# Writing out the loops of an attention and expert kernel, and moving its weight waits and splits to other engines

## The reference

```
x = x + autocorrelation(layernorm(x), ctx, ctx)
x = x + moe(layernorm(x))

autocorrelation, 8 heads of 64 channels, over the 64 positions of each channel:
  corr = ifft(fft(q) * conj(fft(k))).real
  w, idx = top_k(corr, 8);  w = softmax(w)
  out = sum over i of w_i * v shifted by idx_i   (index clamped at the last position)

moe, 16 experts, top 2:
  shared = (silu(x @ Wg.T) * (x @ Wu.T)) @ Wd.T             (512 -> 2 * 512 -> 512)
  two experts of each token by softmax(x @ gate.T), weights normalised to sum 1
  out = sum over both of weight * expert(x) + shared        (expert: 512 -> 2 * 128 -> 512)
```

## Time and profile before

| | us |
|---|---|
| median of 3 runs | 550.24 |
| lowest and highest run | 548.26, 551.55 |
| the profiled execution's own time | 549.62 |
| its span in the trace | 547.8 |
| PE busy | 448.0 (82%) |
| DVE busy | 307.2 (56%) |
| POOL busy | 295.6 (54%) |
| ACT busy | 266.9 (49%) |

### The profile page before, as it was taken

One profiled execution on the slowest core, in us unless ns is written; L12 is line 12 of the kernel. 1 busy time (PEld: TensorE's weight loads), 2 busy tenths in 40 slices (PEclk: granted clock), 3 DMA queues, 4 the chain that ended last, 5 costly groups with the idle time before them and its releaser, 6 DMA issues.

```text
span 547.8 us, 9530 instructions
## 1 busy us (share of the span) xinstructions
PE 448.0 (82%) x2320; PEld 343.5 (63%) x2321; DVE 307.2 (56%) x940; ACT 266.9 (49%) x527; POOL 295.6 (54%) x340
## 2 busy tenths in 40 slices
PE   4699888988988899999905877787777878799995
PEld 3355655655655557788705766676666767588884
DVE  3898989889899836793301322332323323247656
ACT  5688888887888835312002434344444444322120
POOL 3357677777777764097773447474445400056631
PEclk9899999999999999999956999999999999799999
DMA  5522344454542422138876466676666443157854
GB/s 201 245 64 91 121 149 134 134 167 168 184 152 96 155 63 66 46 119 304 283 274 212 145 230 201 210 247 200 219 215 211 125 143 115 40 174 232 251 157 146
DMA packets 39270, 91.58 MB, mean 167 GB/s; under 512 B 4432, under 2 KB 4432, under 8 KB 39120
## 3 DMA queue, kind: packets, MB, share of 16 engines
q1 hardware_dynamic: 32256, 64.31, 35.4%
q0 software_dynamic: 6992, 27.01, 15.1%
HBM read 49.88 MB, written 41.42 MB: 167 GB/s over the span
## 4 chain that ended last, share of the span: by engine, by line
PE 38%; POOL 22%; issue 18%; ACT 8%; DVE 7%; DMA 5%; POOLq 0%; ACTq 0%; DVEq 0%; SPq 0%
PE bank L452 29%; PE bank L602 6%; POOL xs_rows L1251 4%; POOL arena L1167 3%; POOL arena L1170 3%; POOL act_lo L1198 3%; POOL tokens_lo L1154 2%; DMA xg_sb<-xs_rows 2%; POOL rstd L1147 2%; ACT act_lo L721 1%; POOL shw_lo L1202 1%; DMA xs_rows<-x2T,pos_i 1%; ACT arena L776 1%; ACT arena L775 1%; ACT arena L777 1%
## 5 line engine op out<-in xcount | busy, mean ns | idle before, releaser
L1069 DVE TENSOR_TENSOR tokens_lo<-bank,tokens_hi 128x512 fp32r<-128x512 f32 x47 | 32.5, 692 | 89.7 <-ACT tokens_hi L810 89.7
L602 PE MATMUL bank<-const_sb,xg_sb 128*128 128x128 f32 x188 | 31.5, 291 | 58.5 <-issue 38.3
L810 ACT CAST tokens_hi<-bank 128x512 fp32r<-128x512 f32 x47 | 27.6, 587 | 87.8 <-PE bank L602 87.8
L1275 POOL DMA_INDIRECT arena<-y_rows,pos_i x32 | 32.4, 1013 | 66.8 <-DMA y_rows<-sh_act 43.8
L1225 POOL CAST w_hi<-x2T 128x1536 fp32r<-128x1536 f32 x16 | 23.6, 1476 | 74.8 <-PE bank L452 72.2
L602 PEld LDWEIGHTS bank<-const_sb,xg_sb 128*128 128x128 f32 x188 | 20.4, 144 | 68.1 <-issue 67.2
L452 PE MATMUL bank<-tokens_hi,shw_hi 128*128 128x512 f32 x128 | 51.9, 406 | 5.7 <-DVE tokens_lo L878 3.8
L1227 POOL TENSOR_TENSOR w_lo<-x2T,w_hi 128x1536 fp32r<-128x1536 f32 x16 | 55.7, 3481 | 1.3
L452 PE MATMUL bank<-w_hi,tokens_hi 128*128 x188 | 54.1, 288 | 0.2 <-issue 0.2
L452 PE MATMUL bank<-w_hi,tokens_lo 128*128 x188 | 53.5, 285 | 0.0
L452 PE MATMUL bank<-w_lo,tokens_hi 128*128 x188 | 53.5, 284 | 0.0
(11 more groups left out here) (145 smaller groups left out, 1243.6 us busy)
## 6 DMA issues: line engine op xcount, KB each, us to landing
xg_sb<-xs_rows SPq DMA_DIRECT2D x47, 256.0 KB, 2.7
y_rows<-sh_act SPq DMA_DIRECT2D x47, 256.0 KB, 2.1
xs_rows<-act_lo SPq DMA_DIRECT2D x10, 1024.0 KB, 5.1
x2T<-w_exp POOLq DMA_DIRECT2D x13, 768.0 KB, 4.5
resid<-x SPq DMA_DIRECT2D x16, 256.0 KB, 4.7
arena<-ctx SPq DMA_DIRECT2D x16, 256.0 KB, 4.9
x_rows<-arena SPq DMA_DIRECT2D x16, 256.0 KB, 2.1
x2T<-x_rows SPq DMA_DIRECT2D x16, 256.0 KB, 4.2
```

Source lines behind the costliest of these rows:

```text
L602: last = nc.tensor.transpose(ps_xgT[:, cols], xg[b][:, cols], C["identity"])
L810: copy(xgT_halves[b][0], ps_xgT[:, :]).then_inc(xgT_hi_ready, 1)
L1069: tt(lo, ps_xgT[:, :], hi.bitcast(F32), ALU.subtract).then_inc(xgT_ready, 1)
L1275: nc.gpsimd.indirect_dma_start(y_in[buf], None, y_rows[:, :], bass.IndirectOffsetOnAxis(ap=pos_i[:, col:col + 1], axis=0)).then_inc(y_gath ...
```

## The change

- The loops of all engines are written out. `iteration` and `expert` get their numbers as constants.
- The wait for a tile's weights moves from PE to DVE. DVE loads the tile's word (`weights_of`), waits for `w_ready`, and increments a new semaphore `weights_there`; PE waits for that by a constant. It stands at the end of DVE's `expert(n)`, behind the `lo` half of tile n-1's activation (which waits for ACT's `hi` half of it), and is for tile n+1. PE loads a tile's word once and keeps the register for the down product.
- The shared expert's weights are loaded one iteration earlier and are split by POOL alone, in n = 1 to 12: the cast (`split_hi`) behind `keep`, the subtraction (`split_lo`) between the two steps of `odd_product`. The tokens of group 0 are split in the same two places, in n = 13 (tile 0), n = 14 (tiles 1 and 2) and n = 15 (tile 3, here with the cast behind L1189).
- The first three experts' weights are loaded into the place of their own `lo` half, early, and `bounce` is loaded early. POOL splits expert 0 before the scatter, DVE splits experts 1 and 2 beside it. POOL makes the first two `lo` halves of group 0's shared activation, DVE those of group 1's tokens. So the scatter stands behind expert 0's split, instead of behind expert 0's, group 1's tokens' and expert 1's.
- DVE finds the maxima and indices of 15 of the 16 router tiles before the last one's logits are there, and makes the `lo` halves of group 0's third activation behind the positions instead of between their steps.
- POOL loads experts 3 and 4 right behind the scatter (before, behind expert 2's split).
- At the end of the tiles, `shared_half(2, 0, 0)` stands behind the last two down products. The tokens of group 2 are split in four places between tiles 44 and 47 instead of at one.

The diff, cut to its core:

```diff
-                if n == 0:
+                if n == -1:
                     sp.dma_start(shw_in[:, :], shw[:, :]).then_inc(shw_loaded, 16)
...
-            with eng.Fori(hs.start, hs.stop) as h:
-                for b in range(2):
-                    iteration(h, b, None)
+            for n in range(-2, PAIRS + 3):
+                iteration(n // 2, n % 2, n)
...
+            sp.wait_ge(tokens_lo_ready, GT)
+            for t in range(BOUNCES):
+                sp.dma_start(bounce[t], x2_rows[t * P:(t + 1) * P, :]).then_inc(bounced[t], 16)
+            for e, free in enumerate((w_even_psum, out_psum, x2T_psum)):
+                sp.wait_ge(free, PAIRS)
...
+                sp.dma_start(w_raw[e], w_exp[:, e * EXPERT:(e + 1) * EXPERT]).then_inc(weight_first[e], 16)
...
-                pe.wait_ge(w_ready, word % WORD)
+            def gate_up(j, at):
+                b = j % 2
+                pe.wait_ge(weights_there, j + 1)
                 pe.wait_ge(xgT_ready, j + 1)
...
+            def weights_at(j):
+                return pe.value_load(tile_word[0:1, j:j + 1], min_val=1, max_val=(RING - 1) * EXPERT * WORD + E) // WORD
+            def expert(n):
+                b = n % 2
+                if n + 1 < SLOT_TILES:
+                    at[n + 1] = weights_at(n + 1)
+                if n + 2 < SLOT_TILES:
+                    transposes(n // 2 + 1, b)
+                if 1 <= n <= SLOT_TILES:
+                    pe.wait_ge(act_ready, n)
+                    wait(pe, actT_ready, n - 1)
                     nc.tensor.transpose(ps_actT[:, 0:P], act_sb[1 - b][:, :], C["identity"]).then_inc(actT_psum, 1)
+                if n >= 2:
+                    pe.wait_ge(actT_ready, n - 1)
+                    wait(pe, y_ready, n - 3)
+                    down_at = at[n - 2] + KB * 2 * INTER
                     split_product(ps_y[b][:, :], actT_halves[b],
...
+                if n + 1 < SLOT_TILES:
+                    gate_up(n + 1, at[n + 1])
...
-            shared_half(2, 0, 0)
-            for n in range(SLOT_TILES, SLOT_TILES + 2):
-                expert(n // 2, n % 2, n)
+            for n in range(SLOT_TILES + 2):
+                if n == 0:
+                    pe.wait_ge(sh_added, 2 * GT)
+                expert(n)
             for m in range(SB):
                 for part in range(2):
-                    if m or part:
-                        shared_half(2, m, part)
+                    shared_half(2, m, part)
...
-                if n is None or 2 <= n < 2 + SHW // D:
-                    chunk = 2 * h + b - 2
-                    act.wait_ge(shw_loaded, 16)
-                    copy(tile_of(shw_hi, chunk), tile_of(shw_in, chunk)).then_inc(shw_hi_ready, 1)
...
+            def split_weights(e):
+                slot = slice(e * EXPERT, (e + 1) * EXPERT)
+                dve.wait_ge(weight_first[e], 16)
+                dve.wait_ge(w_ready, e)
+                nc.vector.tensor_copy(w_hi[:, slot], w_raw[e]).then_inc(w_hi_ready, 1)
+                dve.wait_ge(w_hi_ready, e + 1)
+                tt(w_lo[:, slot], w_raw[e], w_hi[:, slot].bitcast(F32), ALU.subtract).then_inc(w_ready, 1)
...
-            for t in range(PAIRS):
-                last = nc.vector.max(vals[:, t], log_t[:, t])
+            for tiles in (range(PAIRS - 1), range(PAIRS - 1, PAIRS)):
+                dve.wait_ge(logits_ready, tiles.stop)
+                for t in tiles:
+                    last = nc.vector.max(vals[:, t], log_t[:, t])
...
+            act_lo_split(0, 2)
             shared_multiply(0, 3)
             act_lo_split(0, 3)
+            for t in range(GT):
+                tokens_lo_split(1, t)
...
             for m in range(SB):
                 shared_multiply(1, m)
                 act_lo_split(1, m)
+                if m < 2:
+                    split_weights(m + 1)
...
+            def weights_of(j):
+                word = dve.value_load(tile_word[0:1, j:j + 1], min_val=1, max_val=(RING - 1) * EXPERT * WORD + E)
+                dve.wait_ge(w_ready, word % WORD)
+                dve.sem_inc(weights_there, 1)
...
                     dve.wait_ge(actT_hi_ready, j)
                     hi, lo = actT_halves[1 - b]
                     tt(lo, ps_actT[:, 0:P], hi.bitcast(F32), ALU.subtract).then_inc(actT_ready, 1)
+                if n + 1 < SLOT_TILES:
+                    weights_of(n + 1)
...
+            def split_hi(n):
+                if 1 <= n <= SHW // D:
+                    pool.wait_ge(shw_loaded, 16)
+                    nc.gpsimd.tensor_copy(tile_of(shw_hi, n - 1), tile_of(shw_in, n - 1)).then_inc(shw_hi_ready, 1)
+                for t in split_tokens(n):
+                    pool.wait_ge(x2T_kept, t + 1)
+                    pool.wait_ge(shw_lo_ready, SHW // D)
+                    nc.gpsimd.tensor_copy(tile_of(tokens_hi, t), tile_of(x2T, t)).then_inc(tokens_hi_ready, 1)
...
+            def split_tokens(n):
+                return {PAIRS - 3: (0,), PAIRS - 2: (1, 2), PAIRS - 1: (3,)}.get(n, ())
...
                     nc.gpsimd.tensor_tensor(w_odd_sw, w_odd_sw, ctx_odd_im[pb], ALU.mult).then_inc(odd_im_products, 1)
+                    split_lo(n)
                     pool.wait_ge(out_products_ready, 2 * p + 2)
...
+            pool.wait_ge(xs_zeroed, 16 * (PAIRS - 5))
+            act_lo_split(0)
+            pool.wait_ge(out_products_ready, 2 * PAIRS)
             split_weights(0)
-            for t in range(GT):
-                tokens_lo_split(1, t)
-            split_weights(1)
+            act_lo_split(1)
...
-            split_weights(2)
             for buf in range(BOUNCES):
                 pool.wait_ge(scattered[buf], 16 * CHOICES * PAIRS // BOUNCES)
+            load_weights(4)
+            pool.wait_ge(tokens_lo_ready, 2 * GT)
             load_weights(3)
-            pool.wait_ge(w_ready, 3)
-            load_weights(4)
```

More of the change, by code:

```diff
@@ L331, in segs @@
             return ap.rearrange("p (s l) -> p s l", s=SEGS)
-        def schedule(iteration):
-            for i in range(-2, 4):
-                iteration(i // 2, i % 2, i)
-            return range(2, (PAIRS - 2) // 2), [(i // 2, i % 2, i) for i in range(PAIRS - 2, PAIRS + 3)]
         def live(n, d):
-            return n is None or 0 <= n + d < PAIRS
+            return 0 <= n + d < PAIRS
         def pair(h, b, d):
@@ L429, in _ @@
                 load_xg(j // 2, j % 2)
[L430 to L435 removed]
+            for j in range(6, SLOT_TILES):
+                load_xg(j // 2, j % 2)
+                store_y((j - 6) // 2, j % 2)
+            for j in range(SLOT_TILES - 6, SLOT_TILES):
                 store_y(j // 2, j % 2)
[L437 removed]
+            for t in range(PAIRS):
                 sp.wait_ge(y_added, t + 1)
@@ L832, in _ @@
             act.wait_ge(sh_out_psum, 2 * GT)
-            for n in range(4):
-                expert(n // 2, n % 2, n)
-            with act.Fori(2, SLOT_TILES // 2 - 1) as h:
-                for b in range(2):
-                    expert(h, b, None)
-            for n in range(SLOT_TILES - 3, SLOT_TILES):
-                expert(n // 2, n % 2, n)
-            act.wait_ge(gu_psum, SLOT_TILES)
-            for t in range(GT):
-                tokens_hi_split(2, t)
-            for n in range(SLOT_TILES, SLOT_TILES + 2):
-                expert(n // 2, n % 2, n)
+            for n in range(SLOT_TILES):
+                silu(n)
+                if n + 2 < SLOT_TILES:
+                    gathered_hi(n // 2 + 1, n % 2)
+                if n >= 1:
+                    act_hi_of(n - 1)
+                if n >= 2:
+                    result(n - 2)
+                if n >= SLOT_TILES - 3 and n < SLOT_TILES - 1:
+                    tokens_hi_split(2, n - SLOT_TILES + 5)
+            act.wait_ge(gu_psum, SLOT_TILES)
+            tokens_hi_split(2, 0)
+            act_hi_of(SLOT_TILES - 1)
+            tokens_hi_split(2, 1)
+            result(SLOT_TILES - 2)
+            result(SLOT_TILES - 1)
             for b in range(2):
@@ L1016, in _ @@
             shared_multiply(0, 1)
-            act_lo_split(0, 1)
             dve.wait_ge(counts_psum, 1)
@@ L1082, in expert @@
                     tt(lo, ps_actT[:, 0:P], hi.bitcast(F32), ALU.subtract).then_inc(actT_ready, 1)
+                if n + 1 < SLOT_TILES:
+                    weights_of(n + 1)
             for j in range(2):
                 gathered_lo(0, j)
-            for n in range(4):
+            weights_of(0)
+            for n in range(SLOT_TILES):
                 expert(n // 2, n % 2, n)
-            with dve.Fori(2, SLOT_TILES // 2 - 1) as h:
-                for b in range(2):
-                    expert(h, b, None)
-            for n in range(SLOT_TILES - 3, SLOT_TILES):
-                expert(n // 2, n % 2, n)
+                if n >= SLOT_TILES - 3 and n < SLOT_TILES - 1:
+                    tokens_lo_split(2, n - SLOT_TILES + 5)
             def add_results(quad, u):
@@ L1107, in add_results @@
```

(4 more changed lines are left out.)

192 lines of the change are left out of this document (67 added, 125 removed).

## The result

| | us |
|---|---|
| median of 4 runs | 560.38 |
| lowest and highest run | 559.6, 562.25 |
| ratio to the kernel before | 1.0193, 95% interval 1.0153 to 1.0233 |
| the profiled execution's own time | 560.61 |
| its span in the trace | 558.8 |

The change makes the kernel 1.9% slower. The prediction said 560 us, 62% for slower. How it got there is a matter of each step, and not all of them hold.

A forecast was written before the change was run, and what follows sets the result against it. In the tiles PE's own sequencer was taken as the bound, in attention a cycle of DVE, POOL and ACT. -4.8 + 18.7 - 4.3 = +9.6 on 549.6 us gave 559.2, stated as 560 us; range 535 to 576.

The forecast's parts named there:

- Tiles 2 to 46: Stage of the tiles: gate_up waits for DVE's increment behind ACT's half; 4.15 us a tile against 3.73, +18.7 us.
- the remainder: In a tile, besides the word load: wait, increment, PE's waking and address arithmetic; 0.65 us, bounds 0.2 and 1.0.
- Rival A: Tiles: DVE's sequencer does not stand in PE's way; 3.6 us a tile, 536 us, faster; chance 0.20.
- rival D: Tiles: the word load waits until DVE has finished what is queued; 4.9 us a tile, 593 us; chance 0.07.
- Attention, n = 1 to 13: Attention pairs: POOL's added subtraction costs 6.6 us, less lock, ACT casts and loop edges; sum -1.5 us (-6 to +5).
- Rival C: Attention: POOL goes ahead of L943; 0.75 us more for 12 iterations, 569 us; chance 0.08.
- Tokens of group 0: End of attention: PE waits for the last token split, 6.5 us taken; with attention's part, routing starts 5 us later.
- Positions: DVE's chain before the scatter: -3.0 us for fewer steps, +1 for POOL's expert 0 split beside it; positions at 233.8.
- The scatter: Scatter starts 9.9 us earlier but slows by 8 us (0 to +20) beside DVE's work; its end -1.9 us.
- Rival B: Scatter: DVE cedes the port and the scatter costs nothing more; -8 us, 552 us, no change; chance 0.14.
- Tile 2: First tiles: weight loads issued at once give -2.9 us, so with the scatter's end tile 2's transposes come 4.8 us earlier.
- The end: After the tiles: group 2's tokens split early and down products in the gap shorten PE's wait; -4.3 us (-2 to -6).

The follow-up runs named there:

- the base: The changed kernel with the wait for a tile's weights given back to PE, which loads one word per tile; 521.12 us, run again on another chip 502.21 us.

## Why the prediction was right, point by point

**Tiles 2 to 46: right.** Forecast 4.15 us a tile and +18.7; measured 4.14 and +18.1. The cycle is the one that was written down: ACT's half (ends 1.42 us behind the transposes' start, forecast 1.44), the load, the signalling, `gate_up`. That the sum came out to 0.01 us is luck in part: in the tile shown, from ACT's half to PE's start it is 0.97 us, forecast 0.6 + 0.65, and from there to the next transposes 1.72, forecast 1.45. (The stated bounds of the remainder, 0.2 and 1.0, would give 3.7 and 4.5 us by the same sum, not 3.6 and 4.45.) Doubling the load moved it by its own price, and taking the wait forward removed it. Rival A is excluded by the distances, rival D by the order in time: the load starts at 363.6, ahead of L1066's start at 364.00, so the sequencer runs ahead of DVE's queue.

What the prediction didn't see is the size of the other side. It argued from 3.73 us and gave the change 0.13 us a tile at the best (rival A, 3.6). With its own loop written out and one word PE needs 2.7 to 2.9. The rows held it: PE was busy for 125.6 of 164.0 us, and the waits above put all the rest on its sequencer. So the misplaced wait ate a gain of 44 * (3.73 - 2.85) = 39 us and 18 us more.

**Attention, n = 1 to 13: right in sign and too cautious.** Forecast -1.5, +1.8 of it given back in n = 14; measured -1.3 at the masking of n = 15, where +0.3 was forecast. Taken apart: the second masking is 0.9 us late already, the next 13 distances gain 3.2 us, and n = 14 to 15 loses 1.0 (12.65 for 11.65), forecast 1.8. The mechanism was right (the masking goes first, then the subtraction, then the sum), the term was mis-sized: the sum starts 0.43 us behind its other input (L926 ends at 110.90, L1179 starts at 111.33), not 0.55. Over 12 pairs that is 1.4 of the 1.7 us. Rival C (POOL goes first) is excluded by the same rows. The distance of two maskings was 11.44, forecast 11.6; before it was 11.8, since 11.7 was one distance only, and they alternate between 11.4 and 12.3. What ACT's cast and the loops' edges gave by themselves no run shows.

**Tokens of group 0: the size near, for a reason half wrong.** PE's first matmul on them came at 195.38, forecast near 197. But the tail behind it lost 1.9 us more, so that the last transposes came 6.1 us later, forecast 5. The clock had fallen to half in the wait of 7.00 us; in the base, where it came back sooner, the tail lost 0.6. That the clock is all of it was not shown. The prediction looked for half clock only at the tiles' end.

**Positions: the step that failed.** Forecast -2 for DVE's chain; from the last transposes to the positions it took 20.6 us, 20.2 before, +0.4. "I take +1" for POOL's split beside the chain is the term. It was 3.1 us in L998 alone and 1 us each in L980 and L999, which meet POOL's `act_lo` in the same way, so 5.2 in all. The row for it was there, L1051's 3.60 us, and I took less than a third of it without a reason from a row. What the chain lost in steps was undersized too, 0.4 - 5.2 = -4.8 where -3 was taken, and hides 1.8 of the 4.2 us that the other term missed.

**The scatter: mechanism right, size too large.** Forecast +8; from first to last instruction 44.2 us where 41.2 before, +3.0. The scatter began 3.8 us later than forecast and was 5 us shorter than forecast: two errors that cancel, so its end fell within 1.2 us of the forecast. The longest effect, and beside it that of a cast, POOL's instructions, then DVE's:

```profile
260.53 1.36 POOL L1254 DMA_INDIRECT xs_rows<-x2T,pos_i  x1 [0.31 <-issue]
262.19 2.20 POOL L1254 DMA_INDIRECT xs_rows<-x2T,pos_i  x1 [0.30 <-issue]
```

```profile
260.82 0.95 DVE L847 CAST w_hi<-w_lo 128x1536 fp32r<-128x1536 f32 x1
261.81 1.76 DVE L849 TENSOR_TENSOR w_lo<-w_lo,w_hi 128x1536 fp32r<-128x1536 f32 x1
```

A cast of 0.95 us lengthened an instruction of 0.96 us by 0.40, a subtraction of 1.76 us one by 1.24. "Can cost nearly their length" is what it is at worst. The term that failed is "two thirds of 7 us of L1050 and L1051": those 7 us were their length while POOL held them up (0.94 to 3.60 us each before). Alone, the same six steps took 0.42 us each and lengthened three instructions beside them by 0.1 us each, while the two weight splits, for which the sum has no term, cost 2.6. (The three terms also add up to 7.3, not 8.) Rival B (it costs nothing) is excluded, 44.2 against 41.2, and with a further 2.7 us of DVE it is 45.7.

The Trainium skill (SBUF, State Buffer; section "SBUF: two separate sides") gives 620 ns that became 3100 for such a DMA beside a copy on VectorE. It puts this down to a wait until VectorE's instruction has ended. The trace agrees with the wait: the cast ends at 261.77 us, the instruction beside it at 261.89. It does not agree with a fixed price: a difference of some 2.5 us, as an estimate from the page's two figures, against 0.40 here. The prediction named the rule for a copy and then counted all of DVE's time by it ("about 12 us more"); copies are only the two casts of 0.95 us.

**Tile 2: -2.2, forecast -4.8.** Tile 0's `gate_up` waits, too, for DVE's increment, which stands behind two subtractions of gathered rows: PE starts it at 293.07, 1.9 us behind the end of tile 1's transposes. I had followed the new wait through the loop and not through its first turn. With the wait on PE tile 2 comes 12.2 us behind the scatter's last instruction, in after 14.0, before 13.1; so the early loads, with all else that changed there, are worth 0.9 us, not 2.9.

**The end: -4.9, forecast -4.3.** From tile 46 to the end 81.0 us, 85.9 before; the clock is 1.00 in the row that answers to the second of the earlier trace rows:

```profile
477.80:494.70 16.90, 14.60 (x73) 11.13 (x74) 5.13 (x12) 7.67 (x18) 2.08 (x3) 1.00 0.26 91
```

## What to carry to other kernels

A wait that is moved to another engine takes on everything queued ahead of it there: put it where its inputs are oldest, at the head of that engine's turn, or leave it. Here three places of one wait gave 4.14, 3.13 and 2.92 us a tile, and the last of them is no better than the wait that never moved. Before pricing such a move, read what the freed engine would need with nothing in its way; the gain that the misplaced wait hid here, 39 us, was twice what it cost.

## What the runs showed of the hardware

- POOL's long instructions on SBUF held up DVE's masking (two operands in SBUF) and its copy of 15 columns: 0.17 us became 3.28. They do not hold up everything: DVE's reduction of `top_e` (L917 at 109.01) took 0.20 us in the middle of POOL's L1175. Which one pays depends on which starts first: the masking took 0.68 us when it came ahead of POOL and 1.25 when behind it, and POOL's step 1.73 or 1.28.
- PE was granted 0.51 of its clock for 6 us behind an idle time of 7.00 us (16 matmuls instead of 25), and 0.76 behind one of 7.01 us in the base. In the kernel with early tokens, with no wait longer than 0.6 us there, and in the kernel before, with one of 0.97 us, it was 1.00.
- A load of a word on DVE's sequencer lengthened the tile by 0.57 us, of which the load instruction itself is 0.30; it starts before the vector instructions queued ahead of it are done.
- On one of three chips DVE's products during the scatter began up to 19 us behind the last matmul that they wait for, in four different kernels; the same kernel on another chip had 0.65 us of waiting there. The cause stays open.
